# A second group of nine samples takes the dense path in a two-block network kernel

## The reference

```python
v = (x @ v_w + v_b).reshape(b_, h_, w_, G, C)                 # G = 8 groups, C = 32
deform = (x @ qd_w + qd_b).reshape(b_, h_, w_, G, K, 2)       # K = 9 samples
deform = (deform + prior) * sigmoid(scale) * MAX_SCALE        # MAX_SCALE = 6
weights = (x @ qw_w + qw_b).reshape(b_, h_, w_, G, K)
px, py = ww + deform[..., 0], hh + deform[..., 1]
x0, y0 = floor(px), floor(py)
samp = bilinear(v[b, y0..y0+1, x0..x0+1, g])                  # 0 outside the image
out = einsum('bhwgkc,bhwgk->bhwgc', samp, weights)            # then @ out_w + out_b
```

## Time and profile before

| | us |
|---|---|
| median of 3 runs | 2823.89 (2822.73 to 2824.76) |
| profiled execution, its own time | 2817.64 |
| its span, first to last instruction | 2815.7 |
| busy share: PE, weight loads, DVE, ACT, POOL | 72%, 67%, 69%, 41%, 70% |
| slices of the span (2), busy tenths of POOL | 2, then 7 in each slice until slice 37 |
| mean granted TensorE clock | 0.834 of full |

### The profile page before, as it was taken

How to read it: one execution, slowest core, us unless ns; L and a number is a source line. 1 busy time by engine, 2 the same in 40 slices (tenths; PEclk the granted TensorE clock), 3 DMA queues, 4 the chain that set the end, 5 groups by cost and what they waited for, 6 DMA issues and landing times.

```text
span 2815.7 us, 48893 instructions
## 1 busy us (share of the span) xinstructions
PE 2026.8 (72%) x14272; PEld 1894.5 (67%) x14272; DVE 1940.1 (69%) x3987; ACT 1144.0 (41%) x3544; POOL 1959.2 (70%) x2085
## 2 busy tenths in 40 slices
PE   1465667777777787777778778777777777777578
PEld 1264667767776676676777667677776777677577
DVE  4476677777777777777777777777677777776532
ACT  1222244444434443443434344444434443444355
POOL 2777777777777777777777777777777777777500
PEclk6666789888888888889888888888888888888889
DMA  9622222222221222222222222222112211112100
GB/s 175 160 59 59 66 59 60 64 66 66 67 66 58 63 62 66 66 66 67 59 65 59 66 66 66 65 60 63 53 57 58 59 57 59 57 53 59 50 15 10
DMA packets 263242, 181.03 MB, mean 64 GB/s; under 512 B 188450, under 2 KB 225972, under 8 KB 263188
## 3 DMA queue, kind: packets, MB, share of 16 engines
q0 software_dynamic: 64512, 132.25, 16.2%
q1 hardware_dynamic: 197652, 47.84, 8.3%
q10 hardware_dynamic: 1024, 0.26, 0.0%
HBM read 157.55 MB, written 22.37 MB: 64 GB/s over the span
## 4 chain that ended last, share of the span: by engine, by line
POOL 49%; issue 23%; PE 11%; DVE 10%; ACT 2%; DMA 2%; SPq 1%; DVEq 1%; POOLq 1%; ACTq 0%
POOL got L756 49%; PE Z L1426 3%; PE Y L1436 3%; DVE got L983 2%; PE N L1477 2%; DMA got<-patches,ranks 1%; DVE summed L986 1%; ACT prob L1273 1%; PE N L1335 1%; DVE made L902 1%; SPq L619 1%; ACT hid L1246 1%; DVE turns L1110 1%; PE Y L1434 0%; PE N L1485 0%
## 5 line engine op out<-in xcount | busy, mean ns | idle before, releaser
L756 POOL DMA_INDIRECT got<-patches,ranks x2016 | 1944.0, 964 | 652.3 <-issue 588.6
L1246 ACT ACTIVATE hid<-Z,b 128x128 f32<-128x128 f32 x2048 | 577.2, 369 | 674.1 <-PE Z L1426 673.4
L1436 PE MATMUL Y<-w,hid 128*128 128x128 f32 x4096 | 617.9, 299 | 139.1 <-ACT hid L1246 139.1
L1436 PEld LDWEIGHTS Y<-w,hid 128*128 128x128 f32 x4096 | 563.6, 213 | 154.1 <-ACT hid L1246 145.7
L1426 PE MATMUL Z<-xt_m,w 128*128 128x128 f32 x4096 | 609.8, 301 | 15.5 <-DMA xt_m<-cold_T 15.5
L1426 PEld LDWEIGHTS Z<-xt_m,w 128*128 128x128 f32 x4096 | 576.4, 218 | 21.6 <-issue 17.4
L1335 PE MATMUL N<-ident,made 128*128 128x128 f32 x2304 | 384.3, 324 | 232.4 <-DVE made L902 228.7
L983 DVE TENSOR_TENSOR got<-got,held 128x1152 f32<-128x1152 f32 x224 | 302.3, 1349 | 306.7 <-DMA got<-patches,ranks 302.9
L1335 PEld LDWEIGHTS N<-ident,made 128*128 128x128 f32 x2304 | 319.6, 168 | 270.3 <-DVE made L902 261.9
L986 DVE TENSOR_REDUCE summed<-got 128x32 f32<-128x1152 f32 x224 | 475.1, 2121 | 7.7
L902 DVE TENSOR_TENSOR made<-held,tent 128x1024 f32<-128x1024 f32 x256 | 306.1, 1219 | 10.5 <-PE N L1335 10.4
(11 more groups left out here) (207 smaller groups left out, 2217.6 us busy)
## 6 DMA issues: line engine op xcount, KB each, us to landing
got<-patches,ranks POOLq DMA_INDIRECT x2016, 2.5
vwin<-vpad SPq DMA_DIRECT2D x320, 40.0 KB
patches<-arena SPq DMA_DIRECT2D x92, 128.0 KB
patches<-got SPq DMA_DIRECT2D x38, 128.0 KB, 3.6
w<-in_L_ffn_w SPq DMA_DIRECT2D x2, 2048.0 KB
vpad<-vt SPq DMA_DIRECT2D x128, 16.0 KB
out<-X SPq DMA_DIRECT2D x32, 64.0 KB, 1.6
xt_m<-cold_T ACTq DMA_DIRECT2D x64, 4.0 KB
```

What stands on the lines that cost most here:

```text
L756: pool.indirect_dma_start(out=got[:, q, j * PATCH:(j + 1) * PATCH], out_offset=None, in_=table, in_offset=bass.IndirectOffsetOnAxis(ap=ran ...
L1246: ins = a.activation(hid[:, e % 2, c, :], Z[e % 2][:, c * P:(c + 1) * P], ACT.Relu, bias=b1[n][:, e * FC + c:e * FC + c + 1])
L1436: ins = pe.matmul(Y[:, 0:D], hid[:, e % 2, c, :], w2[n][:, e * FC + c, :], start=False, stop=(e == E - 1 and c == FC - 1))
```

## The change

Groups 6 and 7 take the dense path, as A (samples 0 to 8) and B (9 to 17); six groups are gathered (54 indirect DMAs per tile, parts of four and two groups). Both dense groups use the banks N0 and N1 and `spread`, one after the other, each with its copy and look-up. Tents are made for 18 samples at once, twice as wide. The arrays of the gathered path shrink from 72 samples to 54. The floor is `(p - 0.5 + 1.5 * 2^23) - 1.5 * 2^23`: two instructions for four. In the order, sums k0 to k6 stand in `beside_first` e = 4 to 7; k7, k8, both look-ups and k9 to k17 in `beside_second` e = 0 to 5; `places` goes from `beside_second(3)` to `beside_first(6)`, `corners` from e = 4 to e = 1; `conv(6)` is gone. The table, its stores and the values stored have 6 groups for 8. Before slot 0, nine `make` and seven `sum` run instead of five and four.

Shown: the constants, steps, order, floor and dense parts; left out: the same shrinking in `corners`, in the arena and in the stores, and renamed waits.

```diff
@@ -43,8 +43,12 @@
-DG = G - 1
+DG = G - 2
...
+GJ = DG * K
+KD = GK - GJ
+DC = (G - DG) * C
+MAGIC = 1.5 * 2.0 ** 23
@@ -170,17 +174,17 @@
-        rank = sb("rank", [P, SRING, GK], U32)
-        wq = sb("wq", [P, SRING, GK * CORNERS])
-        spot = sb("spot", [P, SRING, 3, K])
+        rank = sb("rank", [P, SRING, GJ], U32)
+        wq = sb("wq", [P, SRING, GJ * CORNERS])
+        spot = sb("spot", [P, SRING, 3, KD])
...
-        tent = sb("tent", [P, 2, K, W])
+        tent = sb("tent", [P, 2, KD, W])
...
-        v_dense = sb("v_dense", [P, NT, C])
+        v_dense = sb("v_dense", [P, NT, DC])
@@ -245,7 +249,7 @@
-        tents_at, weights_at = 0, (K - 1) * W
+        tents_at, weights_at = 0, K * W
@@ -272,13 +276,14 @@
-        place_v = Steps(sem("place_v"), "xn offs e1 sig off pos clamp spot spotw int flt "
-                "above floor frac frac0 in0 in1 w0 w1 wy wq flc lin rank")
+        place_v = Steps(sem("place_v"), "xn offs e1 sig off pos clamp spot spotw near "
+                "floor frac frac0 in0 in1 w0 w1 wy wq flc lin rank")
...
-        dense_v = Steps(sem("dense_v"), "apart weigh last m0 m1 m2 m3 m4 m5 m6 m7 m8")
-        dense_s = Steps(sem("dense_s"), "abs tent s0 s1 out")
-        dense_t = Steps(sem("dense_t"), "k0 k1 k2 k3 k4 k5 k6 k7 k8 look")
+        ka, kb = (" ".join(f"{{0}}{k}" for k in range(g * K, (g + 1) * K)) for g in range(2))
+        dense_v = Steps(sem("dense_v"), "apart weighA " + ka.format("m") + " weighB " + kb.format("m"))
+        dense_s = Steps(sem("dense_s"), "abs tent sA0 sA1 outA sB0 sB1 outB")
+        dense_t = Steps(sem("dense_t"), ka.format("k") + " lookA " + kb.format("k") + " lookB")
@@ -328,43 +333,45 @@
                     close(u0_before, 0, i - 2)
                 if ends:
                     conv("turn", i - 1, i - 1 + PLEAD if placed else last)
-                dense("make", i, range(5, 6))
-                dense("sum", i, range(4, 5))
+                dense("sum", i, range(7, 9))
+                dense("copyA", i)
+                dense("make", i, range(9, 11))
             if e == 1:
                 if ends:
                     conv("project", i - 1)
                     route("stats", 0, i - 1)
-                dense("make", i, range(6, 8))
-                dense("sum", i, range(5, 6))
+                dense("make", i, range(11, 12))
+                dense("lookA", i)
+                if placed:
+                    places("corners", i - 1 + PLEAD)
             if e == 2:
                 if qk:
                     qkv("stats", i - 2, u0_before)
                 if ends:
                     route("norm", 0, i - 1)
-                dense("make", i, range(8, 9))
-                dense("sum", i, range(6, 8))
+                dense("make", i, range(12, 14))
+                dense("sum", i, range(9, 12))
             if e == 3:
                 if ends:
                     route("turn", 0, i - 1, u0_before)
                 if qk:
                     qkv("norm", i - 2)
-                dense("sum", i, range(8, 9))
-                dense("copy", i)
-                if placed:
-                    places("places", i - 1 + PLEAD)
+                dense("make", i, range(14, 17))
+                dense("sum", i, range(12, 15))
             if e == 4:
+                dense("make", i, range(17, 18))
                 if ends:
                     route("logits", 0, i - 1, u0_before)
                 if qk:
                     qkv("turn", i - 2)
-                if placed:
-                    places("corners", i - 1 + PLEAD)
                 if val:
                     values("norm", i + LEAD)
                 if place:
                     places("norm", i + PLEAD)
-                dense("look", i)
+                dense("sum", i, range(15, 18))
+                dense("copyB", i)
             if e == 5:
+                dense("lookB", i)
                 if ends:
                     route("gate", 0, i - 1)
                 if qk:
@@ -410,47 +417,49 @@
                 if place:
                     places("offsets", i + PLEAD)
                 if tents:
-                    dense("weigh", i + 1)
-                    dense("make", i + 1, range(0, 1))
+                    dense("weighA", i + 1)
+                    dense("make", i + 1, range(0, 2))
                 if final:
                     conv(5, i)
             if e == 4:
                 if att:
                     route("norm", 1, i - 3)
                     route("turn", 1, i - 3, u1, i - 2)
+                if tents:
+                    dense("make", i + 1, range(2, 3))
+                    dense("sum", i + 1, range(0, 2), i - 3 if att else None)
                 if not final:
                     conv(5, i)
-                if tents:
-                    dense("sum", i + 1, range(0, 1), i - 3 if att else None)
                 if final:
-                    conv(6, i)
+                    conv("turn", i, last)
             if e == 5:
                 if att:
                     route("logits", 1, i - 3, u1)
                 if tents:
-                    dense("make", i + 1, range(1, 3))
+                    dense("make", i + 1, range(3, 5))
+                    dense("sum", i + 1, range(2, 4))
                 if final:
-                    conv("turn", i, last)
+                    conv("project", i)
+                    route("stats", 0, i)
             if e == 6:
                 if att:
                     route("gate", 1, i - 3)
-                if not final:
-                    conv(6, i)
                 if tents:
-                    dense("make", i + 1, range(3, 4))
-                    dense("sum", i + 1, range(1, 3))
+                    dense("make", i + 1, range(5, 6))
+                    dense("sum", i + 1, range(4, 5))
+                if place:
+                    places("places", i + PLEAD)
                 if final:
-                    conv("project", i)
-                    route("stats", 0, i)
+                    route("norm", 0, i)
+                    route("turn", 0, i, u0)
             if e == 7:
                 if att:
                     route("count", 1, i - 3)
                 if tents:
-                    dense("make", i + 1, range(4, 5))
-                    dense("sum", i + 1, range(3, 4))
+                    dense("make", i + 1, range(6, 9))
+                    dense("weighB", i + 1)
+                    dense("sum", i + 1, range(5, 7))
                 if final:
-                    route("norm", 0, i)
-                    route("turn", 0, i, u0)
                     route("logits", 0, i, u0)
                     route("gate", 0, i)
 
...
@@ -820,20 +829,17 @@
-            v.tensor_copy(pint, pp).then_inc(*s("int"))
-            v.wait_ge(*d("int", t))
-            v.tensor_copy(fl, pint).then_inc(*s("flt"))
-            v.wait_ge(*d("flt", t))
-            v.tensor_tensor(tmp, fl, pp, ALU.is_gt).then_inc(*s("above"))
-            v.wait_ge(*d("above", t))
-            v.tensor_tensor(fl, fl, tmp, ALU.subtract).then_inc(*s("floor"))
+            pg = p2[:, :, 0:GJ]
+            v.tensor_scalar(fl, pg, -0.5, MAGIC, ALU.add, ALU.add).then_inc(*s("near"))
+            v.wait_ge(*d("near", t))
+            v.tensor_scalar(fl, fl, -MAGIC, None, ALU.add).then_inc(*s("floor"))
...
-            v.tensor_tensor(fr, pp, fl, ALU.subtract).then_inc(*s("frac"))
+            v.tensor_tensor(fr, pg, fl, ALU.subtract).then_inc(*s("frac"))
...
-            w0, w1_ = wlin[:, 0:2 * GK], wlin[:, 2 * GK:4 * GK]
+            w0, w1_ = wlin[:, 0, :, :], wlin[:, 1, :, :]
...
@@ -875,30 +881,28 @@
-            v.wait_ge(*d("m8", t - 1))
+            v.wait_ge(*d(f"m{KD - 1}", t - 1))
...
-                            iota[:, :].unsqueeze(1).to_broadcast([P, 2 * K, W]),
-                            sp3.rearrange("p a k -> p (a k)").unsqueeze(2).to_broadcast([P, 2 * K, W]),
+                            iota[:, :].unsqueeze(1).to_broadcast([P, 2 * KD, W]),
+                            sp3.rearrange("p a k -> p (a k)").unsqueeze(2).to_broadcast([P, 2 * KD, W]),
...
-        if part == "weigh":
+        if part in ("weighA", "weighB"):
+            k0 = "AB".index(part[-1]) * K
...
-            wt = spot[:, bass.ds(t % SRING, 1), 2:3, :].rearrange("p o a k -> p (o a k)")
-            v.tensor_tensor(held[:, tents_at:tents_at + (K - 1) * W].rearrange("p (k w) -> p k w", k=K - 1),
-                            tent[:, 1, 0:K - 1, :], wt[:, 0:K - 1].unsqueeze(2)
-                            .to_broadcast([P, K - 1, W]), ALU.mult).then_inc(*s("weigh"))
-            v.tensor_tensor(tent[:, 1, K - 1, :], tent[:, 1, K - 1, :],
-                            wt[:, K - 1:K].to_broadcast([P, W]), ALU.mult).then_inc(*s("last"))
+            if part == "weighB":
+                v.wait_ge(*d("m8", t))
+            wt = spot[:, bass.ds(t % SRING, 1), 2:3, k0:k0 + K].rearrange("p o a k -> p (o a k)")
+            v.tensor_tensor(held[:, tents_at:tents_at + K * W].rearrange("p (k w) -> p k w", k=K),
```

(62 more changed lines are left out.)

52 lines of the change are left out of this document (26 added, 26 removed).

## The result

The changed kernel takes 2958.91 us (median), the kernel before 2823.31 us on the same chip: ratio 1.0479 (95% interval 1.0458 to 1.0499). Slower was forecast with a chance of 0.62, but by 40 us and not by 135, and the time lies outside the range. (One execution of these four, at 7209 us, and one of the six of e4_floor, at 2941.6 us, are left out everywhere.)

The account below looks back on a forecast made before the run. GpSimd's gathers were taken to set the 81.5 us slot; afterwards VectorE and TensorE in turn, at 84.2 us. Middle slots +70, start, missing values and end bring +39 on 2817.64; with 6.25 to the median, 2863 us, range 2778 to 2925.

Parts of the forecast that it names:

- the four stretches: One slot cut into four consecutive parts: 30.3 + 17.3 + 10.0 + 26.6 = 84.2 us, against 81.5 before.
- down(0), which waits for VectorE's first step of `close`: TensorE's step after k6 and two up-steps, placed at 3.1 us, within 4.7 us ahead of its uninterrupted work.
- stretch I: From the end of k6's outer product to VectorE's `qkv("project")`: grows from 25.5 to 30.3 us, set by TensorE.
- at TensorE's upper clock: The 4.7 us of TensorE work before its 25.6 us in a row were counted at the unthrottled clock.
- the 0.8 us a slot that the second loop was to save: Seven late slots without values were each taken as 0.8 us shorter, 6 us in all.
- III: From the normalised attention weights to the output copy's end: 10.0 us.
- IV: From the output copy's end to the end of k6's outer product: 26.6 us, partly with TensorE at its lower clock.
- B: Rival: TensorE stays at its upper clock as idle times shrink; 81.2 us a slot, 2785 us; chance 0.22.
- E: Rival between the forecast and the upper-clock case: 82.3 to 83.4 us a slot, 2812 to 2843 us; chance 0.15.
- A: The forecast itself: VectorE and TensorE in turn bound the slot at 83.4 to 86 us, 0.7 to 3% slower; chance 0.50.
- C: Rival: GpSimd keeps the pace at 70.3 us a slot, about 2465 us; chance 0.03.
- D: Rival: more waits, above all the ring of three `made` buffers, or ScalarE's tents; 88 us a slot, 2960 us; chance 0.10.

Follow-up runs that it names:

- e4_floor: Kernel before with only the rounding floor, two instructions for four: 2830.99 us, ratio 1.0037.
- e1_head: Changed kernel with the head of VectorE's first slot loop put at slot 0 of an instruction block: 2915.89 us, 1.0333.
- e10: Kernel before with 16 writes to an unused tile added to the loop body, first loop's head at slot 111 of a block: 2819.85 us, 0.9992.
- e2: Changed kernel with `weighB` moved from the end of the loop body to behind the first step of `close`: 2896.23 us, 1.0276.
- e3_gather54: Kernel before without group 6's gathers, product and sum (54 gathers a slot, nothing added): 2492.45 us, 0.8844.
- e5: Changed kernel with both VectorE's loop head at slot 0 of a block and `weighB` behind the first step of `close`: 2892.06 us, 1.0246.
- e9: Kernel before with 16 writes to an unused tile added to the loop body, first loop's head at slot 0 of a block: 2812.76 us, 0.9965.

## Why the prediction was right or wrong

**Right.** GpSimd stops being the bound (70% to 57%), and VectorE and TensorE in turn set a longer slot. Of the four stretches three came out within 0.2 us, and the fourth within 1.0 where no pause falls into it. The waits that were to vanish and to appear did: gathered rows gone (3.8 us of idle time in all before L988), 5.9 us in front of L1099, 2.7 at the projection, and ScalarE's passes over the tents take 1.16 us each. The logits' wait was 1.4 us a slot, not 2 to 3; GpSimd's for `summed` 20.0 instead of 13, as its part of a slot is shorter than the slot by 89.3 - 70.3 = 19.0. The start gained 5.4 us (L1099 of slot 4 at 400.3 for 405.7; forecast 7), and from L1099 of slot 30 to the end it is 19.6 us less (forecast 18 net). So the whole miss lies in slots 4 to 29.

**Wrong: the step "down(0), which waits for VectorE's first step of `close` (three outer products' worth, at 3.1)" in stretch I.** `acc` starts 5.8 us after k6's product, not 3.1 (k6's ends about 1348.1, `acc` starts at 1353.85). Two products and `weighB` take 2.9 us of that, which is near the 3.1; the sum put at nothing the jump between `weighB` and `close`, where the pause of 2.83 us stands. In e1_head, without the fetches, `acc` starts 3.2 us after k6's product. And it continued "at TensorE's upper clock", which did not hold in 13 of 18 slots, because of the same pause. Together pause and clock are worth the 4.4 us by which I falls in e1_head (35.9 to 31.5). Over 18 slots that is 79 of the 102 us by which slots 4 to 29 missed.

The rest has other causes. Without any pause, stretch I is still 31.2 to 31.5 us and not 30.3: from the end of k6's product to the sum of k7 it is 5.1 to 5.3 us for the 4.7 forecast, and from there to `qkv("project")` 26.0 to 26.3 for 25.6. Over 26 slots this makes some 26 us (an estimate from these rows). And the 0.8 us a slot that the second loop was to save for want of values did not come (that loop's slot is 85.3 us against a forecast of 83.4, and I explains 0.9 of it). Small errors of the other sign, in III and IV of the first loop, make up the sum.

The prediction counted VectorE's added instructions only by their durations. That it had 13 more of them in the body of a loop, and that the body came to lie differently, was no term of the sum. The profile before had the row for it, 25 packets of q14, one of them between 480 and 1900 us, but it was not read. The Trainium skill, "Runtime: NRT & Kernel Launch", § Instruction fetch mechanics, says that a jump out of the prefetched instructions forces a fetch by DMA and stalls the engine. The changed kernel, e1_head and e10 agree. They and e2 show besides that with the same code the head's position decides whether there are fetches, and that the work in front of the jump decides how much of the stall is seen.

**The rivals.** B (TensorE stays at its upper clock, 2785) and E (between A and B): wrong; the mean clock rises from 0.834 to 0.878, but IV came out as A had it, and in I the pause brings a new stretch at 1.2 GHz in most slots. C (GpSimd keeps the pace, 2465): wrong; e3_gather54 shows that its number was sound, and that only the added work stood against it. D (88 us a slot, 2960) had the time to 1 us but by luck, not by its mechanism: the ring of `made` buffers costs little (14.0 us in 21 slots before L906), and VectorE's wait for ScalarE's tents is 21.3 us in 22 slots, the 1.0 us that A had in IV. A's mechanism is what e2 and e5 measure, 2896 and 2892 us, inside its 0.7 to 3%; e1 (3.3%) lies just above. It was still 29 us short in e5, from I (+1.0) and III (+0.9) a slot, less 0.7 in IV.

**Still open.** Whether it was the body's length or its new position that made the changed kernel's fetches: a longer body at the old kernel's own position was not tried (e9 chose a good position, e10 a bad one). Whether the overlap of `turns` with a gather causes e4's loss. Why the padded kernel e9 gains 10 us. Why stretch I is some 1 us a slot longer than forecast without any pause.

## What to carry to other kernels

When an edit changes the number of instructions in a loop body, compare the packets of the instruction queues before and after: a number that grows with the trips, and an "issue" idle time at the loop's head, is a price that no list of durations holds. It is cured by the position of the loop's head, or mostly hidden by work without a wait in front of the jump (three outer products in e2; one in e10 was not enough). What it costs depends on the slack behind it: 43 us in the changed kernel, 7 in e10, where GpSimd sets the pace. When the pace passes from one engine to another, the order that suited the old bound has to be done again, several moves together: with it this change is 4.4% faster than the kernel before and not 4.8% slower.

## What the runs showed of the hardware that was not expected

- A jump of VectorE with four instruction fetches of 8 KB around it (a fifth in the middle of the body): 2.8 to 3.1 us of pause, 18 times (52.3 us), and up to 0.82 us more a few instructions on. TensorE, idle meanwhile (3.22 us in the slot shown), falls to 1.2 GHz behind it in 13 of the 18 slots and not in five, and what decides between them is not shown; with that it is 4.4 us a slot in the mean (e1_head). Whether there are fetches depends on the position of the head alone in e9 and e10.
- A gather of 0.94 us takes 1.80 us when a VectorE product of two SBUF operands (1.23 us) starts 0.24 us before it, and always ends 2.04 us after that product's start; it takes 0.94 in the 17 slots of the kernel before where it starts 0.02 to 0.04 us behind the product, and 1.99 in the one where it is 0.05. A kernel (e4_floor) with 0.7 us less work on VectorE a slot became 0.37% slower.
